# A 24-step transformer decoder on one core: in the rotary attention layers, the rotated halves come from a VectorE shuffle and GpSimd products instead of extra TensorE products, and later queries and keys are made between the rounds

## The reference, cut to what matters

```python
def apply_rope(t, freqs):                       # rot = 32 of the 64 features of a head
    t1, tp = (t[..., :rot], t[..., rot:])
    rh = jnp.concatenate([-t1[..., d2:], t1[..., :d2]], axis=-1)      # d2 = 16
    t1 = t1 * jnp.cos(freqs) + rh * jnp.sin(freqs)
    return jnp.concatenate([t1, tp], axis=-1)
def attn_block(xq, ctx, Wq, Wk, Wv, Wo, bo, pe_q, pe_k, mask):        # HEADS = 8, DH = 64
    q, k, v = xq @ Wq, ctx @ Wk, ctx @ Wv       # split into heads
    q = apply_rope(q * DH ** (-0.5), pe_q)
    k = apply_rope(k, pe_k)
    a = jax.nn.softmax(jnp.einsum('bhid,bhjd->bhij', q, k), axis=-1)
    return jnp.einsum('bhij,bhjd->bhid', a, v) ... @ Wo + bo
```

## Time and profile before

| | |
|---|---|
| time, median of 3 executions | 4510.98 us (4506.9 to 4514.82) |
| profiled execution: its time and its span | 4516.42 us; 4514.8 us |
| busy: PE, DVE, ACT, POOL | 4015.5 (89%), 2675.4 (59%), 1998.7 (44%), 860.4 (19%) us |
| mean granted PE clock | 0.955 |
| POOL, line 1505: adds of 128x512; of 128x154 | 192 x 1.27 us; 64 x 0.51 us |
| DVE, lines 365 and 367, 128x512 and 128x154 | 0.68 to 0.69 us; 0.32 us each |
| PE idle before line 738 (XN), ended by DVE's line 365 | 44.7 us in 18 waits |

### The profile page before, as it was taken

How to read it: one execution, slowest core, us unless ns; L and a number is a source line. 1 busy time by engine, 2 the same in 40 slices (tenths; PEclk the granted TensorE clock), 3 DMA queues, 4 the chain that set the end, 5 groups by cost and what they waited for, 6 DMA issues and landing times. The chain is left out here.

```text
span 4514.8 us, 70500 instructions
## 1 busy us (share of the span) xinstructions
PE 4015.5 (89%) x23856; PEld 2483.2 (55%) x23856; DVE 2675.4 (59%) x7163; ACT 1998.7 (44%) x5804; POOL 860.4 (19%) x972
## 2 busy tenths in 40 slices
PE   6887799999999988889968877999999999888898
PEld 4644445655555555555646444565555555555555
DVE  3677566666666644654346775666666666456543
ACT  1732435555445434663227214454554444346632
POOL 2145221122221200000021452211122212000000
PEclk7999999999999998999969999999999999999999
DMA  2000000000000010010010000000000000100000
GB/s 68 24 16 1 16 7 16 22 16 22 16 22 1 25 54 19 7 57 8 1 57 5 16 1 16 7 16 22 16 22 16 22 2 24 54 20 34 30 8 10
DMA packets 15847, 91.84 MB, mean 20 GB/s; under 512 B 2176, under 2 KB 8064, under 8 KB 12032
## 3 DMA queue, kind: packets, MB, share of 16 engines
q1 hardware_dynamic: 15488, 87.27, 5.3%
HBM read 86.22 MB, written 1.05 MB: 19 GB/s over the span
## 5 line engine op out<-in xcount | busy, mean ns | idle before, releaser
L559 PE MATMUL ps_O<-wide,V 128*64 128x256 f32 (+4 forms) x5152 | 596.5, 394 | 1.9 <-ACT wide L583 1.8
L628 ACT ACTIVATE EX<-NB,neg 128x154 f32<-128x154 f32 (+3 forms) x640 | 350.2, 551 | 399.4 <-DVE neg L653 399.2
L601 POOL COPY RX<-recips 128x256 f32<-128x256 f32 (+2 forms) x356 | 156.8, 440 | 1822.9 <-DVE recips L668 1757.2
L679 DVE TENSOR_TENSOR QT<-ps_O,RS 128x512 f32<-128x512 f32 x212 | 146.6, 692 | 444.3 <-PE ps_O L559 444.3
L510 PE MATMUL ps_S<-KT,QT 64*128 64x154 f32 (+7 forms) x1936 | 368.0, 463 | 31.8 <-issue 21.5
L583 ACT ACTIVATE wide<-ps_P 128x512 f32<-128x512 f32 (+2 forms) x648 | 367.6, 569 | 60.9 <-PE ps_P L541 60.8
L394 POOL TENSOR_TENSOR small<-small 128x4 f32<-128x4 f32 x112 | 113.5, 1013 | 1467.8 <-DVE small L379 955.1
L541 PE MATMUL ps_P<-consts,EX 128*128 128x128 f32 (+1 forms) x2148 | 317.3, 281 | 80.0 <-ACT wide L583 41.5
L559 PEld LDWEIGHTS ps_O<-wide,V 128*64 128x64 f32 (+4 forms) x5152 | 266.9, 127 | 194.5 <-issue 110.7
L510 PE MATMUL ps_OUT<-KT,QT 64*128 64x154 f32 (+5 forms) x968 | 336.0, 441 | 0.4 <-ACT EX L628 0.4
L585 DVE COPY wide<-ps_P 128x512 f32<-128x512 f32 (+4 forms) x404 | 259.3, 643 | 117.9 <-PE ps_P L541 117.5
(11 more groups left out here) (345 smaller groups left out, 8154.1 us busy)
## 6 DMA issues: line engine op xcount, KB each, us to landing
weights<-in_w_dram SPq DMA_DIRECT2D x10, 1664.0 KB, 6.8
weights<-in_w_dram SPq DMA_DIRECT2D x2, 6148.0 KB, 17.5
weights<-in_w5next_dram SPq DMA_DIRECT2D x6, 1664.0 KB, 6.8
weights<-in_w_dram SPq DMA_DIRECT2D x2, 4200.0 KB, 13.0
weights<-in_reltab_dram SPq DMA_DIRECT2D x2, 4096.0 KB, 12.3
weights<-in_w_dram SPq DMA_DIRECT2D x8, 640.0 KB, 3.9
weights<-in_w_dram SPq DMA_DIRECT2D x5, 832.0 KB, 4.4
weights<-in_w_dram SPq DMA_DIRECT2D x2, 2050.0 KB, 8.0
```

The source lines that it names most:

```text
L559: ins = pe.matmul(O1[self.slot * j:self.slot * (j + 1), q0 * P:(q0 + self.nq) * P], self.value(c * self.hpc + j, kc), self.probs(rd, j)[:, ...
L601: pool.tensor_copy(RX[:, q0 * P:(q0 + self.nq) * P].rearrange("p (n s) -> p n s", s=self.slot), of.unsqueeze(2).broadcast_to([P, self.nq * ...
L628: ins = act.activation(ex[:, a * N:(a + 1) * N], src, ACT.Exp, bias=neg[:, at:at + 1], scale=-1.0 if self.added else 1.0, accum_out=sums[: ...
L679: dve.tensor_tensor(self.out_chunk(c), O1[:, :], RS[:, c % 2, :], ALU.mult).then_inc(r.av_sb, 1)
```

## The change

The swapped products go. For each chunk DVE now runs a `stream_shuffle` from the product's PSUM bank into the part buffer, which exchanges partitions m and (m + 16) mod 32 in each group of 32, and then the product with cos as before. POOL multiplies the part with sin (line 1581 of the changed kernel; for queries from a new table `sinq`, sin times 0.125, made once) and then adds (line 1583), waiting for its own product between.

The tables are made anew. Self step: keys and queries of chunk 0, the four value products, keys and queries of chunk 1 in front; the keys and queries of chunks 2 and 3 ("late" chunks) one each in iterations 1 to 4. Cross step: the four keys and the queries of chunks 0 and 1 in front; the queries of chunks 2 and 3 in iterations 1 and 2; the two value products stay in `fill`, but with six rows ahead of them the second one now falls on bank O1, and PE waits for ACT's copy of the next step's input out of that bank. A late product takes its turn in the three banks of the rounds (`seq`, letter P). PE makes it ahead of the round's scores, DVE takes it between the second and the third maximum (k == 2), POOL rotates it ahead of the round's spread. The part buffers of a cross step are in `NB`, of a late chunk in a self step in `XN`. The weights `swapq` and `swapk` are still loaded, so the DMAs are the same.

```diff
...
+        sinq = sb("sinq", [P, SEQ])
...
+        HALVES = [(m + 16) % 32 for m in range(32)]
+        def rope(dve, r, bank, dst, part, tables, wait):
+            if wait:
+                dve.wait_ge(*wait)
+            dve.stream_shuffle(part, bank, HALVES).then_inc(r.evac_dve, 1)
+            if tables[0] is None:
+                dve.tensor_tensor(dst, bank, tables[1], ALU.mult).then_inc(r.evac_dve, 1)
+            else:
+                dve.scalar_tensor_tensor(dst, bank, tables[0], tables[1], ALU.mult, ALU.mult).then_inc(r.evac_dve, 1)
...
                 for rd in range(self.rounds + 1):
+                    if rd + 1 in self.late:
+                        self.late_at[rd + 1] = len(self.seq)
+                        self.seq.append(("P", self.late[rd + 1]))
...
             def evacuated(self, eng, r, s):
                 e, n = self.seq[s]
-                eng.wait_ge(r.turned_act if e == "A" else r.turned_dve, n)
+                eng.wait_ge({"A": r.turned_act, "D": r.turned_dve, "P": r.evac_dve}[e], n)
...
                     if i == 1 and fill:
                         fill(pe)
+                    if i in self.late:
+                        if self.late_at[i] >= nb:
+                            self.evacuated(pe, r, self.late_at[i] - nb)
+                        late(pe, i)
...
-            def pool(self, pool, r):
-                for rd in range(self.rounds):
-                    self.spread(pool, r, rd)
+            def pool(self, pool, r, late=None):
+                for i in range(self.steps):
+                    if i in self.late:
+                        late(pool, i)
+                    if 1 <= i <= self.rounds:
+                        self.spread(pool, r, i - 1)
...
-            def dve(self, dve, r, free=None, beside=None):
+            def dve(self, dve, r, free=None, beside=None, late=None):
                 for i in range(self.steps):
                     for k in range(4):
+                        if k == 2 and i in self.late:
+                            late(dve, i)
...
-                self.order = [("k", c) for c in range(4)] + [("q", c) for c in range(4)]
+                if cross:
+                    self.order = [("k", c) for c in range(4)] + [("q", c) for c in range(4)]
+                    at = {1: 6, 2: 7}
+                else:
+                    self.order = [(m, c) for c in range(4) for m in "kq"]
+                    at = {1: 4, 2: 5, 3: 6, 4: 7}
...
-                self.tab = Table([row for j in range(8) for row in self.rotary(j)])
-                self.values = Table(values, self.tab)
+                self.front = Table(ropes if cross else ropes[0:2] + values + ropes[2:4])
+                self.mid = Table(values if cross else [], self.front)
...
+            def before(self, j):
+                if self.cross:
+                    return (self.r.rotated, j - 3) if j >= 4 else None
+                return (self.r.rotated, j) if j >= 5 else None
...
+            def rotate(self, pool, j):
...
+                pool.wait_ge(r.evac_dve, 2 * j + 2)
+                pool.tensor_tensor(part, part, sin, ALU.mult).then_inc(r.sum_step, 1)
+                pool.wait_ge(r.sum_step, j + 1)
+                pool.tensor_tensor(d, d, part, ALU.add).then_inc(r.rotated, 1)
             def pool(self, pool):
...
-                    pool.wait_ge(r.evac_dve, 2 * j + 2)
-                    pool.tensor_tensor(d, d, self.part[j % 4][:, 0:SEQ if m == "q" else self.NK], ALU.add
-                                       ).then_inc(r.rotated, 1)
-                self.att.pool(pool, r)
+                for j in range(8 - len(self.late)):
+                    self.rotate(pool, j)
+                self.att.pool(pool, self.r, lambda pool, i: self.rotate(pool, self.late[i]))
...
                 def fill(pe):
-                    pe.wait_ge(r.evac_dve, self.tab.d)
+                    pe.wait_ge(r.evac_dve, self.front.d)
+                    pe.wait_ge(r.evac_act, self.front.a)
                     self.nxt.pe_head(pe)
-                    pe_table(pe, r, self.values, 0, nv)
...
+                    if self.cross:
+                        pe_table(pe, r, self.mid, 0, 1)
                         pe.wait_ge(self.nxt.r.xT, 1)
-                        pe_table(pe, r, self.values, nv)
...
+                        pe_table(pe, r, self.mid, 1)
...
                 if self.cross:
-                    evacuate(dve, r, self.tab, "D", 0, 8)
+                    evacuate(dve, r, self.front, "D", 0, 4)
                     self.beside(dve, 0)
-                    evacuate(dve, r, self.tab, "D", 8, 12)
+                    evacuate(dve, r, self.front, "D", 4, 5)
                     self.beside(dve, 1)
-                    evacuate(dve, r, self.tab, "D", 12)
+                    evacuate(dve, r, self.front, "D", 5)
                 else:
                     self.beside(dve, 0)
-                    evacuate(dve, r, self.tab, "D", 0, 6)
+                    evacuate(dve, r, self.front, "D", 0, 6)
                     self.beside(dve, 1)
-                    evacuate(dve, r, self.tab, "D", 6, 12)
+                    evacuate(dve, r, self.front, "D", 6)
                     self.beside(dve, 2)
-                    evacuate(dve, r, self.tab, "D", 12)
-                self.att.dve(dve, r, {1: [(r.rotated, 8)]})
+                self.att.dve(dve, r, None if self.cross else {1: [(r.rotated, 4)]}, late=self.late_dve)
...
```

More of the change, by code:

```diff
@@ L344, in evacuate @@
                 if row[3] != who:
+                    continue
+                if row[4] == "rope":
+                    g = tab.j0 + j
+                    eng.wait_ge(r.proj, g + 1)
+                    rope(eng, r, RING[g % len(RING)][0:row[1], 0:row[2]], row[5], *row[6])
                     continue
@@ L450, in __init__ @@
                 self.steps = self.rounds + 2
-                self.seq, self.first = [], []
+                self.seq, self.first, self.late_at = [], [], {}
+                self.late = late or {}
                 done = {"A": 0, "D": 0}
@@ L1476, in __init__ @@
                                      keys=lambda c: KT[:, c, 0:NK],
-                                     queries=lambda c: (self.r.rotated, 4 + c + 1))
-                self.part = [wide[:, 2048 + SEQ * j:2048 + SEQ * (j + 1)] for j in range(4)]
+                                     queries=lambda c: (self.r.rotated, 4 + c + 1 if cross else 2 * c + 2),
+                                     late={i: 2 * j + 2 for i, j in at.items()})
+                ropes = [self.rotary(j) for j in range(8 - len(at))]
@@ L1487, in rotary, with product, tables @@
+            def product(self, j):
+                m, c = self.order[j]
+                return self.w("w" + m)[:, c * P:(c + 1) * P], self.L.XT[:, :] if m == "q" else self.src[:, :]
+            def tables(self, j):
+                m = self.order[j][0]
+                n = SEQ if m == "q" else self.NK
+                return 0.125 if m == "q" else None, K("cos")[:, 0:n]
             def rotary(self, j):
@@ L1489, in rotary @@
                 n = SEQ if m == "q" else self.NK
-                x = self.L.XT[:, :] if m == "q" else self.src[:, :]
-                by = (lambda t: ("times", (0.125, t))) if m == "q" else (lambda t: ("row", (t, ALU.mult)))
-                (kind, cos), (_, sin) = by(K("cos")[:, 0:n]), by(K("sin")[:, 0:n])
-                return [([(self.w("w" + m)[:, c * P:(c + 1) * P], x)], P, n, "D", kind, self.dest(m, c), cos),
-                        ([(self.w("swap" + m)[:, c * P:(c + 1) * P], x)], P, n, "D", kind, self.part[j % 4][:, 0:n],
-                         sin, (self.r.rotated, j - 3) if j >= 4 else None)]
+                return ([self.product(j)], P, n, "D", "rope", self.dest(m, c), (self.part(j), self.tables(j), self.before(j)))
@@ new lines, in late_proj, with late_pe, late_dve @@
+            def late_proj(self, i):
+                return self.mid.j1 + i
+            def late_pe(self, pe, i):
+                j = self.late[i]
+                pe.matmul(self.att.late_bank(i)[:, :], *self.product(j), start=True, stop=True).then_inc(self.r.proj, 1)
+            def late_dve(self, dve, i):
+                j = self.late[i]
+                dve.wait_ge(self.r.proj, self.late_proj(i))
+                rope(dve, self.r, self.att.late_bank(i)[:, :], self.dest(*self.order[j]), self.part(j), self.tables(j),
+                     self.before(j))
@@ new lines, in rotate @@
+            def rotate(self, pool, j):
+                r = self.r
+                m, c = self.order[j]
+                d, part = self.dest(m, c), self.part(j)
+                n = SEQ if m == "q" else self.NK
+                sin = (sinq if m == "q" else K("sin"))[:, 0:n]
+                pool.wait_ge(r.evac_dve, 2 * j + 2)
+                pool.tensor_tensor(part, part, sin, ALU.mult).then_inc(r.sum_step, 1)
+                pool.wait_ge(r.sum_step, j + 1)
+                pool.tensor_tensor(d, d, part, ALU.add).then_inc(r.rotated, 1)
@@ L1538, in act @@
```

(9 more changed lines are left out.)

31 lines of the change are left out of this document (16 added, 15 removed).

## The result

| | before | changed |
|---|---|---|
| median of 4 executions | 4512.15 us (4506.9 to 4514.82) | 4570.17 us (4569.63 to 4572.04) |
| ratio | | 1.0131 (95% interval 1.0113 to 1.0148) |
| span profiled, mean granted clock | 4514.8 us, 0.955 | 4570.4 us, 0.938 |
| self step, lane 0; lane 1 | 71.37; 71.31 us | 69.42; 70.10 us |
| cross step, lane 0; lane 1, means of 8 | 42.99; 43.19 us | 47.90; 47.84 us |

The changed kernel is 58 us slower (forecast: 50). The steps account for it: 16 cross steps lose 4.8 each, 76 us; 16 self steps gain 1.6 each, 25 us. That is +51 of the 55.6 by which the spans differ; the rest lies in steps that the change doesn't touch.

A forecast was written before the change was run, and what follows sets the result against it. PE was taken to bound both kinds of step. 16 x (4.5 - 2.1) = +38 and +11 for clock, together +50 on 4516, gave 4566, less 5 for the median: 4561 us, range 4475 to 4630.

The forecast's parts named there:

- Forecast A: Whole kernel: POOL's chain and the four engines' order in rounds set PE's pace; 4561 us, range 4530 to 4630, chance 0.70.
- Removed: PE in both steps: products and a bank wait go, 6.9 us a self step, 4.5 a cross step, 182 in all.
- Shuffle and rotation: DVE and POOL: shuffle 0.61 us start to start, 0.69 to the end; rotation of 512 2.67, short rotation 1.12.
- Self step, front: Before round 2 of a self step: waits of 1.1 and 1.2 us, yet round 2 starts 6.8 earlier, at 18.4.
- Self step, rounds: From round 2 of a self step: two late products of 0.86 and three bank waits of 0.9 cost 4.4 us.
- The slipping norm: DVE's four norm products in a self step slip in one per POOL boundary, ending at about 8.6 instead of 6.1.
- Cross step: PE idles 10 us for the rotation; the step ends 5.3 us later in lane 0, 3.6 in lane 1, mean 4.5.
- Clock drops in self steps, 0.7 x 16 = 11: Front waits of self steps drop the clock, 1.7 us each in four of ten steps: +11 us with rounding.
- Rival B: Self and cross rounds hide the late chunks, PE not meeting the late product's bank: 84 us less, 4477 us, chance 0.19.
- Rival C: The clock; its claim and size are not in the text given; chance 0.09.
- Rival D: Products come off whole with nothing late: 4329 us; needs a cross step's `rotated` at t 2.9; chance 0.02.
- Signs listed beforehand: Changed profile: PE busy down about 180 us, POOL up 277, scores idle about 160, cross step 47 to 48, self about 69.

The follow-up runs named there:

- run 10: Changed kernel with late chunks, cross products, values and norm reordered, plus self-step chunk 1 made ahead of the values and evacuated ahead of the norm: 4432.61 us, 0.9834.
- run 11: As run 10, but in self steps POOL rotates chunk 1 only when the norm's products are done: 4395.7 us, 0.9742.
- run 6: Changed kernel, but PE fills its wait in each cross step with ten extra products of 512 that nothing reads: 4571.32 us, 1.0123.
- run 3: Changed kernel, but VectorE takes a late chunk ahead of the round's first two maxima instead of behind them: 4508.79 us, 0.9994.
- run 4: Changed kernel, but cross steps make keys and queries in pairs and GpSimd rotates the first two ahead of the next norm's power: 4571.52 us, 1.013.
- run 7: Changed kernel, but a cross step's two value products are made in front, while PE waits for the rotation: 4521.41 us, 1.0014.

## Why the prediction was right, step by step

- **Forecast A held**: 4570 against 4561. The sum was +38 for the steps and +11 for clock; the steps gave +51 and the clock of self steps nothing. Mechanism and order came as written; that the total is 9 us off and no more is partly luck, since errors of both signs cancel (below).
- **Removed**: 182 us of PE work foreseen, PE's busy time fell by 149.5. By steps, the 16 self steps lose 95 us of it (110 foreseen) and the 16 cross steps 60 (72 foreseen); steps without a change have 6 more. In self steps the clock is 1.00 throughout but for the first of each pass; there four late products at 0.95 to 1.06 from start to scores (851.71 to 852.66, 865.46 to 866.52) instead of 0.86 are some 0.7 of the 0.9 that is missing in each. In cross steps PE works 3.3 to 6.3 us behind its wait at the lower clock, and what runs there counts longer.
- **Shuffle and rotation**: the shuffle was taken as 0.61 from start to start and 0.69 to the end. It measures 0.62 and 0.73, so the term was right. (The upper bound mixed two bases, 1.38 less 0.69; from start to start it is 1.38 less 0.61, 4660 instead of 4649.) The key in the cross step takes 0.51 for product and add each and 1.05 with the gap between (984.97 to the next key at 986.02; taken 1.12), the queries take 2.66 (taken 2.67). POOL's busy time rose by 277.1, as written.
- **Self step, front**: round 0 at 7.9 (8.0), fill wait 0.98 (1.2), third item 0.77 (0.7), round 2 at 18.38 (18.4). The wait of 0.4 in front of the next late product did not come.
- **Self step, rounds**: here a term was too small. "2 x 0.86 + 3 x 0.9 = 4.4" was 4.85. A late product in the middle of a round costs 1.06, not 0.86 as in a row of products; the waits are 0.83. So 2 x 1.06 + 3 x 0.83 = 4.6, with 0.25 that I can't place. Lane 1 waits 1.34 for round 0 instead of 0.80. The gain is 1.95 and 1.21 where 2.4 and 1.85 stood: 34 us foreseen in all, 25 found.
- **The slipping norm**: its four products took 4.11 in the self step. Three of them end 0.14 to 0.15 behind the end of an operation of POOL (845.66, 846.93 and 848.28; POOL's end at 845.52, 846.78 and 848.13), and the fourth, with POOL idle, takes 0.34: they slip in one per boundary, as in the sum. In run 10 (5.10) all four end so, in run 11 (2.00) one does.
- **Cross step**: round 0 at 12.15 (12.9), round 1 at 19.8 (20.1), round 2 at 25.4 (25.8), the step 4.9 longer in lane 0 (5.3). The 1.5 from round 0's scores to VectorE's first maximum, a part of the 18.4 for XT, was the author's estimate, and no run before the change shows it: the change took 1.40 (992.04 to 993.44) at a granted clock of 0.50, run 6 took 0.83 (992.17 to 993.00) at 1.00. The 0.3 in which VectorE was to slip between POOL's operations didn't delay POOL, whose four keys and first queries took 6.93 (984.97 to 991.90) where 4.5 + 2.67 stood. In lane 1 I took off 1.7 for a lower clock in the old time. The trace of before already had the price of such a drop: its cross steps at the upper clock take 42.88 to 42.90 us, those with a drop, in both lanes, 43.1 to 43.4. So the term was too large by more than 1 us: 4.65 found, 3.6 foreseen. Mean 4.8, foreseen 4.5.
- **Clock drops in self steps, 0.7 x 16 = 11**: wrong. Lane 1 takes 70.08 to 70.10 us in every layer, and none falls; only the first self step of each pass has a drop, as it had before. The two errors, 11 too much here and 9 + 4 too little above, all but cancel. What lies beyond the steps' 51, 4.3 in the spans and 7 in the medians, the forecast did not have.
- **Rival B** named its own condition, VectorE taking the late chunk ahead of the maxima: run 3 makes exactly that, 61 us off where its price was 84. **Rival C**, the clock, with a chance of 0.09, did not come: the clock is low in round 0 and at the value products of every cross step (0.50 from 992 to 998 in the one shown), but back before round 1 in all 16 (its scores take 0.79), and 14 of 16 self steps have no drop. It costs 0.7 to 1.0 a cross step (run 6), since most of the lower clock runs beside ACT's chain: the wait for XT ends at 17.69 in the change and at 17.03 with the clock up. **Rival D** had the right reason against it in the unchanged order; run 11, with the order changed, is still 67 us above its 4329.
- **Signs listed beforehand**: POOL-ended idle time 178.6 us (about 160), waits of 0.83 in rounds, POOL's busy time, a slower line 430 (mean 0.74 for 0.50), cross 47.8 to 48.2 us, self 69.4 and 70.1 came. PE's busy time fell less (149.5 for 180). PE's wait for XT came with 0.35 to 1.23 in the 16 cross steps, but these are 11 us in all and not one of the two largest groups; the second new one is the late product's bank, 75 us.

## What to carry to other kernels

Work taken from the bounding engine pays only where the operands of what follows are ready sooner; list the late ones in their order, since behind the first (a rotation on POOL) a second of nearly the same height may stand (a norm on DVE), and moving the first alone can gain nothing (run 4). Put what waits for nothing into the idle time (run 7, 49 us), and let the engine that holds a bank serve it before its own larger work (run 3, 61 us): with these and the norm's new place the same products, shuffles and rotations give 0.974 instead of 1.013. A drop of PE's clock has no one price: it cost 0.2 to 0.5 us a cross step before, 0.7 to 1.0 in the change, 2 in run 4 and 1.6 in run 6, according to where in the step it fell. Where DVE's operations from SBUF run against a stream of POOL, let POOL pause for them if its results are needed later: the four products of the norm took 5.10 in the stream and 2.00 with the pause, and in run 11 that took 2.6 us off a self step.

## What was not expected of the hardware

- A late product between value products and scores costs 1.06 from its start to the scores (865.46 to 866.52), where a row of such products goes at 0.86. Why, the runs don't say.
- DVE operations with a PSUM source weren't held by POOL: a shuffle of 512 out of PSUM takes 0.72 to 0.74 and the product behind it 0.67 to 0.68, with POOL idle or in its stream. The norm's product, from SBUF alone, is 0.34 at its shortest and 1.42 at its longest.
- With ten extra products in the idle time the clock is up to the next wait (1.00 from 983 to 997.1 in run 6), but behind a wait of 2.2 us it is then lower in 6 of 16 steps (the value product takes 1.99, at 0.50 from 1044.2 on) and not in the other 10 (1.08). What tells them apart stays open.
